# An expert loop on one core: two TensorE signals for each expert, tokens turned two experts ahead, the scatter ahead of the gather

## The reference

```
scores = softmax(xf @ gate_w.T)                      # 64 experts
_, idx = top_k(scores + gate_b, 6)                   # 6 experts for each token
xb[e, pos] = xf[tok]                                 # at most 128 tokens for each expert
h  = silu(xb[e] @ w1[e].T) * (xb[e] @ w3[e].T)       # 176 hidden values
yb = h @ w2[e].T
y[tok] += yb[e, pos] * weight                        # each token's 6 results
z = silu(xf @ ws1.T) * (xf @ ws3.T) @ ws2.T          # the shared expert
out = y + z
```

## Time and profile before

| | |
|---|---|
| median of 3 timed runs | 633.22 us |
| lowest and highest | 632.42 and 634.51 us |
| span of the profiled execution, first to last instruction | 671.0 us |
| TensorE busy in the span | 545.3 us, 81% |
| VectorE, ScalarE, GpSimd busy | 439.3, 358.8, 218.8 us |
| mean granted TensorE clock | 0.908 of full speed |
| expert loop, first to last w13 product | 435.7 to 636.9 us |

### The profile page before, as it was taken

One profiled execution on the slowest core, in us unless ns is written; L12 is line 12 of the kernel. 1 busy time (PEld: TensorE's weight loads), 2 busy tenths in 40 slices (PEclk: granted clock), 3 DMA queues, 4 the chain that ended last, 5 costly groups with the idle time before them and its releaser, 6 DMA issues.

```text
span 671.0 us, 9955 instructions
## 1 busy us (share of the span) xinstructions
PE 545.3 (81%) x3242; PEld 438.7 (65%) x3242; DVE 439.3 (65%) x995; ACT 358.8 (53%) x894; POOL 218.8 (33%) x230
## 2 busy tenths in 40 slices
PE   3969760565546999999999999999889789888976
PEld 3737650133236899999998878776556557566675
DVE  4987998999994455555555137575646646654576
ACT  1667624355546677777773464255545645565610
POOL 2010001134226011111112312566656666666400
PEclk9977985668857999999999999999979989998878
DMA  8960000054000000000000020056646657565583
GB/s 279 382 235 0 1 0 0 0 194 133 2 0 1 24 25 25 24 25 25 1 1 1 1 68 9 18 169 180 183 135 197 169 147 212 163 204 166 144 363 104
DMA packets 43894, 67.31 MB, mean 100 GB/s; under 512 B 11022, under 2 KB 27015, under 8 KB 43716
## 3 DMA queue, kind: packets, MB, share of 16 engines
q1 hardware_dynamic: 36868, 64.62, 30.3%
q0 software_dynamic: 6976, 2.07, 1.5%
HBM read 66.81 MB, written 17.20 MB: 125 GB/s over the span
## 4 chain that ended last, share of the span: by engine, by line
PE 56%; DVE 26%; ACT 6%; issue 5%; another core or an unknown queue 3%; DMA 1%; POOL 1%; SPq 0%; ACTq 0%; DVEq 0%
PE ps L1089 9%; PE ps L736 6%; PE ps L734 6%; PE ps L735 6%; PE ps L953 5%; PE ps L911 4%; PE ps L942 4%; PE ps L741 3%; PE ps L1097 2%; PE ps L925 2%; PE ps L1079 2%; DVE region L1731 2%; PE ps L1136 2%; DVE region L1742 1%
## 5 line engine op out<-in xcount | busy, mean ns | idle before, releaser
L1089 PE MATMUL ps<-region 128*128 128x352 f32 x256 | 93.0, 488 | 5.9 <-issue 3.1
L694 POOL DMA_INDIRECT y_rows<-region x60 | 62.2, 1037 | 58.1 <-ACT region L1433 39.1
L1787 DVE TENSOR_TENSOR region<-ps,region 32x136 f32<-32x136 f32 x128 | 38.1, 297 | 60.1 <-PE ps L911 58.6
L685 POOL DMA_INDIRECT region<-x_rows,region x64 | 68.1, 1064 | 20.2 <-issue 17.4
L734 PE MATMUL ps<-nTh,high 128*128 128x272 f32 (+2 forms) x248 | 74.1, 299 | 0.4 <-ACT region L1362 0.4
L735 PE MATMUL ps<-nTl,high 128*128 128x272 f32 (+2 forms) x248 | 71.7, 289 | 0.0
L644 POOL COPY region<-region 32x544 f32<-32x544 f32 x32 | 26.4, 825 | 122.2 <-DVE region L1806 120.7
L1456 ACT ACTIVATE high<-region 88x512 fp32r<-88x512 f32 x64 | 40.3, 630 | 43.2 <-remote 23.1
L1089 PEld LDWEIGHTS ps<-region 128*128 128x128 f32 x256 | 45.7, 199 | 24.5 <-issue 7.3
L1935 DVE SCALAR_TENSOR_TENSOR region<-region,ps 128x176 f32<-128x176 f32 x64 | 25.3, 396 | 53.3 <-ACT region L1446 24.4
L736 PE MATMUL ps<-nTh,pairs_low 128*128 128x272 f32 x192 | 55.4, 289 | 0.0
(11 more groups left out here) (264 smaller groups left out, 1439.3 us busy)
## 6 DMA issues: line engine op xcount, KB each, us to landing
region<-moe_w SPq DMA_DIRECT2D x64, 352.0 KB
region<-moe_w SPq DMA_DIRECT2D x64, 176.0 KB
y_rows<-zrow SPq DMA_DIRECT2D x1, 6528.0 KB, 25.3
region<-y_rows SPq DMA_DIRECT2D x8, 768.0 KB, 10.7
region<-wqkv SPq DMA_DIRECT2D x8, 384.0 KB, 3.0
region<-ffn_w SPq DMA_DIRECT2D x2, 1024.0 KB, 8.3
region<-patches SPq DMA_DIRECT2D x3, 384.0 KB, 8.3
region<-patches SPq DMA_DIRECT2D x1, 1152.0 KB, 10.7
```

What stands on the lines that cost most here:

```text
L685: nc.gpsimd.indirect_dma_start(out=xb[m8], out_offset=None, in_=x_rows, in_offset=bass.IndirectOffsetOnAxis(ap=sloti[:, at:at + 1], axis=0 ...
L694: nc.gpsimd.indirect_dma_start(out=y_rows, out_offset=bass.IndirectOffsetOnAxis(ap=sld[m8], axis=0), in_=yb[m], in_offset=None, bounds_che ...
L1089: mm = nc.tensor.matmul(ps[:, 2 + m % 2, 0:2 * EI], xbT[m % 2][:, c, :], w13[m][:, c, :], start=(c == 0), stop=(c == DC - 1))
L1787: last = V.tensor_tensor(sc[r, s0:s0 + 8, 0:T].rearrange("p (a b) t -> p a b t", a=4), ps[r, 4:8, 0:4 * GW].rearrange("p a (b h t) -> p a ...
```

## The change

The three TensorE signals after an expert's w13 product become one, s_step, set by the last matmul of each step. Three small functions give its count: `tokens_turned`, `hidden_turned` and `rows_made`. Within a TensorE step the order becomes: w13 product of expert n, hidden rows of expert n - 1, row products of expert n - 2, then the tokens of expert n + 2. Spreads and placings carry no signal of their own in the loop and move to steps 2, 4, 6 and 0 of a group; shared tiles 6, 7 and 8 move to steps 0 and 1 of the loop. The turned hidden rows alternate between banks 4 and 1. ScalarE begins a step with the Silu, then makes w2's high part for expert n - 1, and then copies hidden rows, tokens and rows (of expert n - 2). VectorE follows, with the slot work at the end of a step and the late masks four experts earlier. GpSimd scatters before it gathers, and a gather waits only for the table (once in eight) and, for the first eight experts, for its semaphore. The rest of the diff renames semaphores and gives the spreads and placings ahead of the loop their signals at the call.

```diff
+    return e + 1
+def hidden_turned(e):
+    return e + 4
+def rows_made(e):
+    return e + 5
 class Region:
...
 s_xpk = sem("s_xpk")
@@ -460,6 +473,7 @@
 SUM_BANK = [0, 1, 2, 3, 4, 6, 5, 7, 0]
 PE_TILES = (1, 3, 5)
 MIX_BANK = [2, 3, 4, 5, 6, 7, 0, 1, 2]
+HT_BANK = (4, 1)
 def ln_bank(k, g):
@@ -537,7 +551,7 @@
                      A["moe_w13"][bass.ds(e, 1)].rearrange("e p c n -> p (e c) n")).then_inc(s_w13[m], 16)
     def load2(e, m):
-        need(sp, s_y, e - 3)
+        sp.wait_ge(s_step, rows_made(e - 4))
         sp.dma_start(w2[m], A["moe_w2"][e] if isinstance(e, int) else
                      A["moe_w2"][bass.ds(e, 1)].rearrange("e p c n -> p (e c) n")).then_inc(s_w2[m], 16)
...
@@ -678,10 +692,10 @@
         m = m8 % 4
         at = EB * (b % 2) + m8
-        pool.wait_ge(s_tab, b + 1)
-        need(pool, s_xtb, e - 7)
-        need(pool, s_sld, e - 7)
-        need(pool, s_got[m], 4 * (e - 4 - m) + 16)
+        if m8 == 0:
+            pool.wait_ge(s_tab, b + 1)
+        if e < EB:
+            need(pool, s_got[m], 4 * (e - 4 - m) + 16)
         nc.gpsimd.indirect_dma_start(
             out=xb[m8], out_offset=None, in_=x_rows, in_offset=bass.IndirectOffsetOnAxis(ap=sloti[:, at:at + 1], axis=0),
             bounds_check=last_token, oob_is_err=False).then_inc(s_got[m], 16)
@@ -696,10 +710,10 @@
             bounds_check=last_row, oob_is_err=False).then_inc(s_add[m], 16)
     def pool_step(n, b, m8):
+        if 0 <= n - 3 < E - LATE:
+            put(n - 3, (m8 - 3) % EB)
         if 5 <= n + 5 < E:
             gather(n + 5, b + (m8 + 5) // EB, (m8 + 5) % EB)
-        if 0 <= n - 3 < E - LATE:
-            put(n - 3, (m8 - 3) % EB)
     for e in range(3):
         gather(e, 0, e)
...
+    def turn_hidden(e, k):
+        pe.wait_ge(s_eh, e + 1)
+        need(pe, s_ehl, e - 1)
+        for c in range(2):
+            mm = nc.tensor.transpose(ps[0:EH, HT_BANK[k % 2], c * P:(c + 1) * P], eh[k % 2][:, c * EH:(c + 1) * EH],
+                                     ident[:, :])
+        return mm
+    def second_product(e, k):
+        pe.wait_ge(s_ehl, e + 1)
+        pe.wait_ge(s_w2l, 2 * (e + 1))
+        need(pe, s_yb, e - 1)
+        if e < 2:
+            pe.wait_ge(s_h4, 7 + 2 * e)
+        if e - 1 > E - LATE:
+            pe.wait_ge(s_late, e - 1 - (E - LATE) + LATE)
+        for c in range(2):
+            mm = product(ps[:, 5 + 2 * (k % 2), 0:D], (ehT_h[k % 2][:, c, :], ehT_l[k % 2][:, c, :]),
+                         (w2_h[k % 2][:, c, :], w2_l[k][:, c, :]), c == 0, c == 1)
+        return mm
     def pe_step(n, b, m8):
         m = m8 % 4
-        if 0 <= n + 1 < E:
-            e, k = n + 1, (m + 1) % 4
-            pe.wait_ge(s_got[k], 4 * (e - k) + 16)
-            need(pe, s_xbT, e - 1)
-            for c in range(DC):
-                mm = nc.tensor.transpose(ps[:, k % 2, c * P:(c + 1) * P], xb[(m8 + 1) % EB][:, c * P:(c + 1) * P],
-                                         ident[:, :])
-            mm.then_inc(s_xtb, 1)
+        last = None
         if n == 0:
             pe.wait_ge(s_h4, 6)
         if 0 <= n < E:
@@ -1089,39 +1123,39 @@
                 mm = nc.tensor.matmul(ps[:, 2 + m % 2, 0:2 * EI], xbT[m % 2][:, c, :], w13[m][:, c, :],
                                       start=(c == 0), stop=(c == DC - 1))
             mm.then_inc(s_eh13, 1)
-        if 0 <= n - 1 < E:
-            e, k = n - 1, (m - 1) % 4
-            pe.wait_ge(s_eh, e + 1)
-            need(pe, s_ehl, e)
-            for c in range(2):
-                mm = nc.tensor.transpose(ps[0:EH, 4, c * P:(c + 1) * P], eh[k % 2][:, c * EH:(c + 1) * EH],
-                                         ident[:, :])
-            mm.then_inc(s_ehtr, 1)
+        if n == 0:
+            pe.wait_ge(s_hsh, 3 * CH)
+            pe.wait_ge(s_slot, 2)
+            shared_rows(6, 5)
+            shared_rows(7, 6)
+        if 0 <= n - 1 < E - 1:
+            last = turn_hidden(n - 1, (m - 1) % 4)
+        if n == 1:
+            shared_rows(8, 7)
         if 0 <= n - 2 < E:
-            e, k = n - 2, (m - 2) % 4
-            pe.wait_ge(s_ehl, e + 1)
-            pe.wait_ge(s_w2l, 2 * (e + 1))
-            need(pe, s_yb, e - 1)
-            if e - 1 > E - LATE:
-                pe.wait_ge(s_late, e - 1 - (E - LATE) + LATE)
-            for c in range(2):
-                mm = product(ps[:, 5 + 2 * (k % 2), 0:D], (ehT_h[k % 2][:, c, :], ehT_l[k % 2][:, c, :]),
-                             (w2_h[k % 2][:, c, :], w2_l[k][:, c, :]), c == 0, c == 1)
-            mm.then_inc(s_y, 1)
-        if m8 < 3 and 0 <= n < E - 2 * EB:
-            q, c = b + 2, m8
+            last = second_product(n - 2, (m - 2) % 4)
+        if n == E:
+            last = turn_hidden(n - 1, (m - 1) % 4)
+        if m8 in (2, 4, 6) and 0 <= n < E - 2 * EB:
+            q, c = b + 2, m8 // 2 - 1
             if c:
                 pe.wait_ge(s_val, 3 * q - 4 + c)
             else:
                 pe.wait_ge(s_tab, q)
+                if b == 0:
+                    pe.wait_ge(s_h4, 8)
             spread_groups(6, q, c)
-        if m8 == 3 and 0 <= b < 3:
-            pe.wait_ge(s_val, 3 * b + 5)
-            second_shared(6 + b, 6)
-        if m8 == 5 and 0 <= n < E - 2 * EB:
-            if b < 3:
-                pe.wait_ge(s_h4, 7 + b)
-            place_slots(b + 2)
+        if m8 == 0 and EB <= n < E - EB:
+            place_slots(b + 1)
+        if 0 <= n + 2 < E:
+            e = n + 2
+            pe.wait_ge(s_got[e % 4], 4 * (e - e % 4) + 16)
+            need(pe, s_xbT, e)
+            for c in range(DC):
+                last = nc.tensor.transpose(ps[:, 0, c * P:(c + 1) * P], xb[e % EB][:, c * P:(c + 1) * P],
+                                           ident[:, :])
+        if last is not None:
+            last.then_inc(s_step, 1)
     run_steps(pe_step)
     pe.wait_ge(s_yb, E)
...
@@ -1425,35 +1459,33 @@
     def act_step(n, b, m8):
         m = m8 % 4
-        if 0 <= n - 3 < E:
-            e, k = n - 3, (m - 3) % 4
-            act.wait_ge(s_y, e + 1)
+        if 0 <= n < E:
+            act.wait_ge(s_eh13, n + 1)
+            need(act, s_eh, n - 1)
+            nc.scalar.activation(es[m % 2], ps[:, 2 + m % 2, 0:EI], ACT.Silu).then_inc(s_es, 1)
+        if 0 <= n - 1 < E:
+            e, k = n - 1, (m - 1) % 4
+            act.wait_ge(s_w2[k], 4 * (e - k) + 16)
+            if e >= 2:
+                act.wait_ge(s_step, rows_made(e - 2))
+            nc.scalar.activation(w2_h[k % 2], w2[k], ACT.Copy).then_inc(s_w2h, 1)
+            act.wait_ge(s_step, hidden_turned(e))
+            nc.scalar.activation(ehT_h[k % 2], ps[0:EH, HT_BANK[k % 2], 0:2 * P].rearrange("p (c n) -> p c n", c=2),
+                                 ACT.Copy).then_inc(s_ehT, 1)
+        if 0 <= n + 2 < E:
+            e, k = n + 2, (m + 2) % 4
+            act.wait_ge(s_step, tokens_turned(e))
+            nc.scalar.activation(xbT[k % 2], ps[:, 0, 0:2 * P].rearrange("p (c n) -> p c n", c=DC),
+                                 ACT.Copy).then_inc(s_xbT, 1)
+        if 0 <= n - 2 < E:
+            e, k = n - 2, (m - 2) % 4
+            act.wait_ge(s_step, rows_made(e))
             if e < E - LATE:
                 need(act, s_add[k], 4 * (e - 4 - k) + 16)
                 nc.scalar.activation(yb[k], ps[:, 5 + 2 * (k % 2), 0:D], ACT.Copy).then_inc(s_yb, 1)
             else:
                 nc.scalar.activation(y_parts[e - E + LATE][:, 0, :], ps[:, 5 + 2 * (k % 2), 0:D],
                                      ACT.Copy).then_inc(s_yb, 1)
-        if 0 <= n + 1 < E:
-            e, k = n + 1, (m + 1) % 4
-            act.wait_ge(s_xtb, e + 1)
-            need(act, s_eh13, e - 1)
-            nc.scalar.activation(xbT[k % 2], ps[:, k % 2, 0:2 * P].rearrange("p (c n) -> p c n", c=DC),
-                                 ACT.Copy).then_inc(s_xbT, 1)
-        if 0 <= n < E:
-            act.wait_ge(s_eh13, n + 1)
-            need(act, s_eh, n - 1)
-            nc.scalar.activation(es[m % 2], ps[:, 2 + m % 2, 0:EI], ACT.Silu).then_inc(s_es, 1)
-        if 0 <= n - 1 < E:
-            e, k = n - 1, (m - 1) % 4
-            act.wait_ge(s_ehtr, e + 1)
-            need(act, s_y, e - 1)
-            nc.scalar.activation(ehT_h[k % 2], ps[0:EH, 4, 0:2 * P].rearrange("p (c n) -> p c n", c=2),
-                                 ACT.Copy).then_inc(s_ehT, 1)
-        if 0 <= n < E:
-            act.wait_ge(s_w2[m], 4 * (n - m) + 16)
-            need(act, s_y, n - 1)
-            nc.scalar.activation(w2_h[m % 2], w2[m], ACT.Copy).then_inc(s_w2h, 1)
     run_steps(act_step)
...
     dve.wait_ge(s_logit, 1)
@@ -1883,13 +1916,15 @@
     def widen_slots(q):
-        need(dve, s_tabps, q)
+        if q < 2:
+            need(dve, s_tabps, q)
         V.tensor_tensor(wide8, bc(best8, 1, SG), bc(lay8[:, EB:EB + SG], 2, EB), ALU.mult).then_inc(s_wide, 1)
     def keep_slots(q):
         at, to = EB * q, EB * (q % 2)
-        dve.wait_ge(s_tabps, q + 1)
+        if q < 2:
+            dve.wait_ge(s_tabps, q + 1)
```

(56 more changed lines are left out.)

34 lines of the change are left out of this document (18 added, 16 removed).

## The result

The changed kernel took 639.21 us (median of 18 runs) against 634.00 us for the kernel before (18 runs): ratio 1.0081, 95% interval 1.0063 to 1.0100. Ratios here leave out the few runs of a kernel that took over 1.5% longer than its fastest, and they can differ by some 0.2% from the quotient of the medians given beside them. The forecast was 637.5, slower. The profiled execution of the changed kernel is one of these runs: 639.52 us, its span 637.3.

A forecast was written before the change was run, and what follows sets the result against it. TensorE and GpSimd were taken as level bounds before (592.5 and 592.6 us), GpSimd as the bound after. 633.2 + 6.6 (GpSimd's later start and order) − 2.3 (end) = 637.5 us; range 626.5 to 641.5.

The forecast's parts named there:

- The start: Loop start: shared tiles 6, 7 and 8 in steps 0 and 1 put scatter 0 at 447.3, 4.0 us later.
- Two issues more, 2.65 us: GpSimd's order: scatter before gather makes 111 issues from scatter 0 to gather 63, not 109, costing 2.65 us.
- The pair of 2.65 us: GpSimd's loop turn: one gather and one scatter take 2.65 us, scatter to scatter, when nothing holds it.
- Landing, 2.2 us: GpSimd's indirect transfers: one lands about 2.2 us after its start; it could be 1.5 or 3.5.
- TensorE's floor of 156.8 us: TensorE's own loop work before: first w13 product at 435.72, the last could start at 592.5; quiet steps of 2.35 us.
- The end, −2.3 us: After the last w13 product: chain to the first late sum falls from 9.2 to 6.9 us, gaining 2.3 us.
- the late signals "belong nearly all to the profiled execution": TensorE's signals in the loop: late in the profile, with at most 6.6 us left for them in the timed runs.
- Pricing the signals at nothing: TensorE's fewer signals in the loop: no gain in the timed runs, between 0 and 6.6 us.
- rival 2: TensorE's signals are late in the timed runs too, up to 6.6 us; time 628 us; chance 0.21.
- Rival 1: GpSimd's pair takes 2.50 us without the profiler, only the end's gain counts; time 630.9 us; chance 0.27.
- rival 3: Hidden chain in each loop step overshoots: shared signal 0.9 us late costs 0.1 in some 55 steps; 643 us; chance 0.08.
- Rival 4: Signals fewer but as late, number not the cause; profile near 660, time 637.5 us; chance 0.44 together with the forecast.

The follow-up runs named there:

- tiles_place: Changed kernel, placing of slots one step later and three shared tiles moved from steps 0 and 1 into 51, 53 and 55: 634.13 us, 1.0053 of before.
- both_place_b: Changed kernel, placing one step later, three shared tiles into steps 51 to 55, gather before scatter: 632.93 us, 1.0023; as both_place on a late chip 668.4 us, 0.9990.
- scatter_sp: Changed kernel with the 60 scatters issued by SyncE as plain transfers of the same 128 rows to fixed places: 631.59 us, 1.0004 of before.
- before_half: Kernel before with the scatters of odd experts left out, on a late chip: 634.32 us, 0.9456 of before.
- after_again: Changed kernel once more, nothing edited, on the second late chip: 674.65 us, 1.0079 of before.
- place_later: Changed kernel with one edit, the placing of slots one step later, on the quick chip: 639.13 us, 1.0125 of before.
- both: Changed kernel, gather ahead of scatter again and three shared tiles moved from steps 0 and 1 into 51, 53 and 55, late chip: 673.32 us, 1.0061 of before.

## Why the prediction was right, and where it was not

**Slower, by about what was said.** 4.3 us forecast (633.2 to 637.5), 5.2 measured. The mechanism, GpSimd as the loop's bound, is shown: it issues without a pause, TensorE waits for gathers late in the loop, and with its scatters gone the loop shortens by 5.6 us.

**The start.** Scatter 0 was put at 447.3 and came at 447.82, of which 0.5 is a later first product (436.21 for 435.72). Taking the tiles away gives back 3.9 us at scatter 0 and 5.0 of the time, a difference of medians that is good to some 3 us; the term was 4.0. Right.

**Two issues more, 2.65 us.** Over-priced. The order gave 1.2 us in the time and 1.3 at gather 63, and the intervals tell the 1.2 neither from zero nor from 2.65. With the tiles gone, TensorE's own pace is close as well, which would hide a part of the gain: the last w13 product starts 165.3 us after the first one in tiles_place and 165.7 in both_place_b, and 163.8 in scatter_sp, where TensorE never waits for a gather.

**The pair of 2.65 us.** The usual pair is that; the mean is not. From scatter 0 to gather 63 (447.82 to 599.47) there are 111 issues: 1.366 us each, 2.73 a pair. Of the 115 spacings from scatter 0 on, 23 are over 1.4 us and hold 5.2 us more than 1.33 each would; the longest, 2.08 us, is the one from 595.83 to 597.91 above. Gather 63 was due at 594.4 and came 5.1 later, 0.5 of it with the start. The earlier trace rows had shown the spread, and the sum used the middle.

**Landing, 2.2 us.** Too short for most gathers under load. Of the changed kernel's gathers (L699, last line of its view):

```profile
DMA to landing us min/median/max: 2.1/3.8/5.5
```

The one that TensorE last waited for was not gather 63, as the prediction had it, but gather 62, turned 5.11 us after its start; gather 63 itself landed in 2.1 us, while TensorE was busy. The last w13 product comes 6.5 us later than forecast (605.66 for 599.2): 5.1 by gather 63's start, the other 1.4 by this. The span is 637.3 for 631. The sum was short by 6 us in the profile and by only 1.7 in the time, because it started from the measured 633.2: both terms would lengthen a loop of before that is bound by GpSimd too, and so cancel in the difference. No trace shows that loop of before, so how well they cancel is in part luck.

**TensorE's floor of 156.8 us** (435.72 to 592.5) was too low for the changed kernel: 163.9 in scatter_sp, of which 4.0 are the placing's waits, put at 0 to 3. The rest is about what the slot work costs more than it was priced at: from w13 product to w13 product a quiet step of scatter_sp takes 2.34 us, one with a full spread 2.80, with a short one 2.62, with a placing 3.43. So a spread costs 0.46 (put at 0.31), a short one 0.28 (0.10), a placing 0.43 beside its wait (0.28).

**The end, −2.3 us.** The chain measured 6.95 us against 6.9 forecast; in before_half the old one is 9.4 (601.00 to 610.38). The whole stretch behind the last w13 product takes 31.6 us in the changed kernel, 30.5 to 32.9 in its versions, and 34.1 and 33.8 in before and before_half. Right.

**The wrong step: the late signals "belong nearly all to the profiled execution".** They don't. Some 2 us lie around a span, in every run, and on the late chips the timed runs of before are at 670 like the span of 671.0. That trace is of such a chip, by its length, its late signals and its 4712 signal records, while the 633.2 came from another kind. The two were never of one condition, and their difference of 37.8 us was not what profiling costs. Whether the taking of records has a part in the late signals stays open all the same: every run of the experiments lists a span and a granted clock, so none is known to be without records, and the traces of the late kind lack a third of them. The Trainium skill ("NOTIFIC — the notification-queue block", section 7.1, Overflow) says that a full queue of records, in one of its settings, stalls the engine that makes them. No run here tests it. What the runs do show is that the execution whose trace was kept doesn't stand out: that of after_again took 680.48 us and is one of seven, from 671.35 to 681.15. Pricing the signals at nothing where before needs 634 came out for another reason: on such a chip none is late in any trace of the changed kernel and its versions. It follows that rival 2 fell, as far as those traces go. Rival 1 (a GpSimd turn of 2.50) fell with the mean of 2.73; rival 3 fell too: the step's shared signal came on time, and inside the loop TensorE waited for the hidden rows in hardly any steps but those of a moved placing (0.41 us). Rival 4 was right on the late chips in its first half, that the number of signals is not the cause.

**What stays open.** The terms as measured (5.0 and 1.2 slower, 2.3 faster) make 3.9 us; the change costs 5.2 in the result, and 8.1 in place_later on the quick chip. both_place_b has the old start, the old order and the shorter end, and by this account would be 2.3 us below before, 0.9964; its interval begins at 0.9994. Some 2 to 4 us that the kernel before saves in its loop are unaccounted for, and no trace of before on a quick chip exists to find them. scatter_sp says where to look: with GpSimd's bound taken away and the shorter end it is still no faster than before (1.0004). If the lead-in and the end are as above, the loop of before there is an estimated 161 to 162 us (163.8 less 0.6 in the time and some 2 at the end), below TensorE's own 163.8 in the changed kernel. So the new order on TensorE, with the placing's waits in it, seems to cost some 2 us that the prediction put at nothing. This is worked out from differences of medians, not shown by a trace. Nor do I know why the ratio on a late chip (1.0079) is that of the result. There the placing may count: both, without the placing moved, has 1.0061 and both_place 0.9990, but on two chips, alike in the time of before, and with intervals that just touch. No version here beats the kernel before.

## What to carry to other kernels

Before reasoning from a trace, hold its own execution's time against the timed runs: a difference of 6% can mean another condition of the machine, as here, and then only the structure of the trace counts. Count its signal records as well: here a third fewer of them marked the same chips. Where an engine issues back to back, price its turn by the mean over the whole run (2.73 us here), not by the usual one (2.65), and a landing by those under load (3.8, not 2.2). Work put into the first steps of a pipeline delays for good an engine that never pauses afterwards: three tiles of 1.29 us in steps 0 and 1 put scatter 0 back by 3.9 us and gather 63 by 5.1. And a wait that one moves is gone only when the next trace shows no new one in its place.

## What the runs showed of the hardware

On the two late chips TensorE's signals arrived late, by up to 3.2 us in after_again and 4.7 in the trace of before, and mostly while GpSimd issues indirect transfers back to back: from the fourth in a row on, 75 of 82 signals of before and 27 of 32 of after_again, against 0 of 111 on the chip of the result. ScalarE's and VectorE's signals in the loop of after_again were on time, as far as they have a record (about 60% do). The same kernel takes 670 us there and 631 to 634 elsewhere; leaving out 30 of 124 indirect transfers took 35 us off there. The traces there hold a third fewer signal records. What makes the difference between the chips, no run shows.

An indirect transfer of 128 rows took GpSimd 1.02 us and a pause of 0.30, a mean of 1.37 us from start to start over 111 of them, and a gather landed 2.1 to 5.5 us after its start (median 3.8). After an idle time of 1.70 us of TensorE the granted clock was 0.57 for the 4 us that followed, and the step took 1.5 us longer.
